# An attention and lookup block on one core: the first two heads' q and k loads reordered, split and spread

## What is computed

```python
x = x + layernorm(attention(layernorm(x)))     # 16 heads, D = 16, softmax over 4096 keys
x = x + layernorm(lookup_ffn(layernorm(x)))    # top 8 of 1024 keys, gated

def attention(x):                              # all in float32
    q, k, v = split(x @ w_qkv + b_qkv)
    attn = softmax((q @ k.T) * D ** -0.5)      # one 4096 x 4096 matrix a head
    return (attn @ v) @ w_proj + b_proj
```

## Time and profile before

| | us |
|---|---|
| median of 3 runs | 3294.21 |
| the runs | 3290.62, 3294.21, 3294.38 |
| the profiled execution | 3291.98 |
| its span | 3290.2 |

### The profile page before, as it was taken

One profiled execution on the slowest core, in us unless ns is written; L12 is line 12 of the kernel. 1 busy time (PEld: TensorE's weight loads), 2 busy tenths in 40 slices (PEclk: granted clock), 3 DMA queues, 4 the chain that ended last, 5 costly groups with the idle time before them and its releaser, 6 DMA issues.

```text
span 3290.2 us, 80364 instructions
## 1 busy us (share of the span) xinstructions
PE 3136.5 (95%) x27243; PEld 1406.9 (43%) x27243; DVE 2824.3 (86%) x3108; ACT 2514.8 (76%) x4551; POOL 262.0 (8%) x810
## 2 busy tenths in 40 slices
PE   8799999999999999999999999999999999988983
PEld 3444443444344434444444344434444444456662
DVE  5389998999899989998999899989999999456666
ACT  6158888888888888888888888888888888733333
POOL 2300000000000000000000000000000000011113
PEclk9689999999999999999999999999999999989996
DMA  7700101010110001010101010101010101000001
GB/s 255 90 1 1 30 11 27 14 27 14 21 21 21 21 18 24 18 24 15 27 11 30 8 33 8 33 5 37 5 37 5 36 1 30 1 0 0 0 0 51
DMA packets 27384, 83.26 MB, mean 25 GB/s; under 512 B 4641, under 2 KB 15633, under 8 KB 24018
## 3 DMA queue, kind: packets, MB, share of 16 engines
q1 hardware_dynamic: 26818, 77.84, 10.7%
q0 software_dynamic: 272, 1.05, 0.1%
HBM read 57.90 MB, written 20.97 MB: 24 GB/s over the span
## 4 chain that ended last, share of the span: by engine, by line
PE 94%; DVE 2%; issue 2%; ACT 1%; DMA 1%; POOL 1%; DVEq 0%; SPq 0%; POOLq 0%; ACTq 0%
PE ps L1023 41%; PE ps L1034 35%; PE ps L1253 4%; PE ps L998 3%; PE ps L1044 2%; PE ps L1202 2%; PE ps L957 2%; PE ps L1242 1%; PE ps L1177 1%; PE ps L971 1%; PE ps L1052 1%; PE ps L949 1%; DMA q_stack<-qk_parts 1%; ACT q_raw L619 1%; PE ps L1219 0%
## 5 line engine op out<-in xcount | busy, mean ns | idle before, releaser
L750 DVE TENSOR_REDUCE partial<-ps 128x1 f32<-128x1024 f32 x2048 | 2460.7, 1223 | 202.5 <-PE ps L998 158.5
L569 ACT ACTIVATE work<-ps 128x512 f32<-128x512 f32 x4096 | 2203.9, 598 | 383.0 <-PE ps L1023 173.9
L998 PE MATMUL ps<-k_stack,q_stack 48*128 48x512 f32 x4096 | 1509.4, 449 | 25.3 <-DMA q_stack<-qk_parts 17.0
L1023 PE MATMUL ps<-q_stack,k_stack 64*128 64x512 f32 x4096 | 1508.2, 448 | 18.8 <-issue 17.8
L1034 PE MATMUL ps<-work,v_head 128*32 128x256 f32 x16384 | 1304.4, 393 | 0.0
L1023 PEld LDWEIGHTS ps<-q_stack,k_stack 64*128 64x128 f32 x4096 | 633.0, 185 | 814.4 <-ACT work L569 695.6
L998 PEld LDWEIGHTS ps<-k_stack,q_stack 48*128 48x128 f32 x4096 | 622.6, 187 | 55.6 <-DVE partial L750 31.9
L1034 PEld LDWEIGHTS ps<-work,v_head 128*32 128x32 f32 x16384 | 330.9, 108 | 702.6 <-issue 436.8
L415 POOL CAST nm_parts<-negmax 128x4 bf16<-128x4 f32 x128 | 24.7, 193 | 2256.1 <-DVE negmax L757 2255.2
L1253 PE MATMUL ps<-k_raw,q_raw 128*128 128x256 f32 x512 | 126.3, 403 | 17.8 <-ACT q_raw L619 17.8
L619 ACT ACTIVATE q_raw<-ps 128x1024 f32<-128x1024 f32 x32 | 32.8, 1024 | 131.4 <-PE ps L1242 131.4
(11 more groups left out here) (128 smaller groups left out, 1137.4 us busy)
## 6 DMA issues: line engine op xcount, KB each, us to landing
k_stack<-qk_parts SPq DMA_DIRECT2D x96, 256.0 KB, 4.2
q_stack<-qk_parts SPq DMA_DIRECT2D x96, 256.0 KB, 4.2
qk_parts<-qk_part SPq DMA_DIRECT2D x32, 512.0 KB, 2.8
x_sb<-L_attn_x SPq DMA_DIRECT2D x8, 512.0 KB, 11.1
out<-work SPq DMA_DIRECT2D x8, 512.0 KB, 2.9
k_raw<-L_ffn_aux_values SPq DMA_DIRECT2D x1, 1024.0 KB
work<-L_attn_w_qkv POOLq DMA_DIRECT2D x1, 768.0 KB, 7.4
q_raw<-L_ffn_aux_keys SPq DMA_DIRECT2D x1, 512.0 KB
```

Source lines behind the costliest of these rows:

```text
L569: act.activation(probs[:, g % DEPTH, i, :], ps[:, bank, :], ACT.Exp, scale=SCALE).then_inc(exp_done, 1)
L750: dve.tensor_reduce(partial[:, k // 4, k % 4:k % 4 + 1], ps[:, 2 * slot:2 * slot + 2, :], AX.XY, ALU.max).then_inc(max_used, 1)
L998: last = pe.matmul(ps[:, 2 * slot + e, :], q_stack[HALF:HALF + ROWS, b1, c * CH + (k // 4) * P:c * CH + (k // 4 + 1) * P], k_stack[HALF:HA ...
L1023: pe.matmul(ps[:, bank, :], k_stack[0:HALF, b, P * tile:P * (tile + 1)], q_stack[0:HALF, b, at:at + CH], start=True, stop=True).then_inc(s ...
```

## The change

The first head's twelve loads are issued by a new function, `load_first`, in another order: slots 3, 4 and 5 (the maxima's rows) of both stacks first, counted on a new semaphore `first_max_in`, then slots 0, 1 and 2, counted on `first_score_in`. SP issues them after waiting for `parts_out[0]` and `parts_out[2]` only, and waits for `parts_out[1]` and `[3]` behind them. TensorE waits for `first_max_in` ahead of the first maxima and for `first_score_in` ahead of the first score unit. The second head's loads no longer follow at once: each waits on `pv_done`, the first for one finished unit of head 0's first iteration, each further one for two more. As the first head no longer counts on `stack_in[1]`, the loop's wait for it is one head lower.

```diff
--- before.py
+++ after.py
@@ -206,6 +206,8 @@
         v_evac = sem("v_evac")
         v_biased = sem("v_biased")
         stack_in = [sem(f"stack_in{b}") for b in range(NB)]
+        first_max_in = sem("first_max_in")
+        first_score_in = sem("first_score_in")
         s_ready = sem("s_ready")
         exp_done = sem("exp_done")
         m_ready = sem("m_ready")
@@ -296,19 +298,25 @@
                     dst = parts_dram[g // 2, :, (g % 2) * P:(g % 2 + 1) * P, bass.ds(c * CH, CH)]
                     sp.dma_start(dst.rearrange("r f t -> f r t"), qk_part[:, g, :, :]).then_inc(parts_out[g], 16)
 
-            for g in range(4):
-                sp.wait_ge(parts_out[g], 16 * (NC + 1))
-
-            def load_stack(h, b, after=None):
+            def load_first(slots, done):
+                for n in slots:
+                    for stack, qk, part in ((k_stack, 1, SLOT_K[n]), (q_stack, 0, SLOT_Q[n])):
+                        sp.dma_start(stack[SLOT_ROW[n]:SLOT_ROW[n] + D, 1, 0:T].bitcast(F32),
+                                     parts_dram[qk, part, 0:D, :]).then_inc(done, 16)
+
+            def load_stack(h, b, after):
                 for n, (row, pq, pk) in enumerate(zip(SLOT_ROW, SLOT_Q, SLOT_K)):
                     for m, (stack, qk, part) in enumerate(((k_stack, 1, pk), (q_stack, 0, pq))):
-                        if after is not None:
-                            sp.wait_ge(pv_done, after + (2 * n + m) * LOAD_EVERY)
+                        sp.wait_ge(pv_done, after + (2 * n + m) * LOAD_EVERY)
                         sp.dma_start(stack[row:row + D, b, 0:T].bitcast(F32), parts_dram[qk, part, h * D:(h + 1) * D, :]
                                      ).then_inc(stack_in[b], 16)
 
-            load_stack(0, 1)
-            load_stack(1, 0)
+            for g in (0, 2, 1, 3):
+                sp.wait_ge(parts_out[g], 16 * (NC + 1))
+                if g == 2:
+                    load_first((3, 4, 5), first_max_in)
+                    load_first((0, 1, 2), first_score_in)
+            load_stack(1, 0, 1 + CREDIT[pv_done])
             for h in range(2, H):
                 load_stack(h, (h + 1) % NB, (h - 1) * PAIRS * KG + CREDIT[pv_done])
 
@@ -1123,7 +1131,7 @@
                        (b, PAIRS - 1, chunks_ahead(b, PAIRS - 1)))
                 attend(first + (PAIRS - 1), b, PAIRS - 1, chunks_ahead(b, PAIRS - 1), (1 - b, 0, chunks_ahead(1 - b, 0)))
 
-            pe.wait_ge(stack_in[1], 16 * LOADS)
+            pe.wait_ge(first_max_in, 16 * LOADS // 2)
             for c in range(AHEAD):
                 for k in range(16):
                     for e in range(2):
@@ -1139,11 +1147,12 @@
             max_row(1, S_BANK[-1 % SRING])
             pe.wait_ge(vhead_ready, 1)
             pe.wait_ge(rows_set, 2)
+            pe.wait_ge(first_score_in, 16 * LOADS // 2)
             for g in range(LAG):
                 unit(g, 0, 1, 0, chunks_ahead(1, 0), None)
             with pe.Fori(0, H // NB - 1) as r:
                 next_loaded(r * NB, 1, r + 1)
-                next_loaded(r * NB + 1, 0, r + 2)
+                next_loaded(r * NB + 1, 0, r + 1)
             next_loaded(H - 2, 1, H // NB)
 
             def transpose_weights():
```

## The result

| | before | after |
|---|---|---|
| median, us | 3294.38 (6 runs, 3290.62 to 3295.13) | 3275.94 (6 runs, 3266.65 to 3277.40) |
| profiled execution, its span | 3291.98, 3290.2 | 3277.40, 3275.6 |

The ratio of after to before is 0.9941, 95% interval 0.9928 to 0.9954. The forecast was 3276.3.

A forecast was written before the change was run, and what follows sets the result against it. TensorE, busy 95% of the span, bounds the kernel, with 17.0 us idle awaiting the first loads. Cutting that by 15.6 us plus 0.9 us of clock gives 16.5, from 3292.8 to 3276.3 us; range 3270.5 to 3283.

The forecast's parts named there:

- Step 1: First head's loads: the maxima's six go first, the sixth landing 16.15 us after first issue; 13.9 us without the early issue.
- Step 2: SP's waits before the first head's loads: waiting for groups 0 and 2 only moves the first issue 1.7 us earlier.
- Step 3: Score rows' six loads: land 14 us later, at 114.4, at no cost, with 60 us of cover.
- Step 4: Second head's loads, spread over the first iteration: last issue near 243.4, price 0, cover 19 us.
- Step 5: TensorE's clock at the start of the maxima: first four matmuls take half of 2.07 us, gain 0.9 us.
- The sum: Whole change: 15.6 us of shorter TensorE idling plus 0.9 us of clock, 16.5 us.
- The fit: DMA skill page's transfer formula: twelve loads would take an estimated 9 us, so the change would give 0.
- B: Rival at the first loads: half of the gain, slower landings and 4 us lost to ScalarE or clock, 3283; chance 0.10.
- C: Rival at the first loads: twelve share the queue, only 1.7 us of early issue is left, 3291; chance 0.03.
- D: Rival at the third iteration: second head's loads late, TensorE waits 22 us plus 3.4 of clock, 3302; chance 0.02.
- A: Rival in the maxima: clock stays high, up to 24 us more gain, half priced, 3264; chance 0.07.

The follow-up runs named there:

- e1: Kernel before with only the new order and split of the first head's loads; median 3278.86 us, ratio to before 0.9965.
- e2: Kernel before with only the early issue, the first head's loads going out after groups 0 and 2; median 3292.02 us, ratio to before 1.0004.
- e3: Kernel before with only the second head's loads spread over the first iteration; median 3293.23 us, ratio to before 1.0000.
- e8: Changed kernel with the second head's loads let out nine units later; median 3282.98 us, ratio to before 0.9974.
- e6: Changed kernel with q's first 1024 columns of the maxima's rows loaded ahead of the other 3072; median 3273.60 us, ratio to before 0.9940.
- e11: Changed kernel with k's first two slots of each set loaded by one 512 KB transfer on 32 partitions instead of two; one run, 3273.89 us.
- e4: Changed kernel without the spreading, the second head's loads issued at once; median 3275.92 us, ratio to before 0.9948.
- e5: Changed kernel with each v unit among the maxima cut into two halves; median 3275.70 us, ratio to before 0.9934.
- e7: Changed kernel with both halved v units and q's first 1024 columns loaded first; median 3255.24 us, ratio to before 0.9889.
- e9: The kernel of e7 run again for more executions; median 3246.75 us, ratio to before 0.9869.

## Why the prediction was right

**Step 1**, order and split, was right and is most of the gain: e1. The sixth landing came 16.3 us after the first issue (86.72 + 14.1 against 84.46), where 16.15 was forecast.

**Step 2**, the early issue, was over-sized. The issue did move (84.46 against 86.05, with a profile that runs 0.2 us late), but only 1.0 us of the 1.7 reaches TensorE in e2, and 1.5 us between e1 and after. The prediction put the other bound at 0 and was right to keep one.

**Step 3** held: the score rows landed at 89.49 + 25.0 = 114.5, 62 us ahead of the first score at 176.2. (The prediction's "next 62 us" on the maxima's rows alone are 192.74 - 116.11 = 76.6 us by the earlier trace rows; nothing in the sum uses them.)

**Step 4** held: last issue at 243.83 (243.4 forecast), combines 41.3 us apart with the loads in the first iteration, no wait ahead of the third; e3 gives the price as 0 and e8 the cover.

**Step 5**, the clock. The 0.9 us is there: four maximum matmuls took 1.19 us and not 2.07. The v units before the wait were also faster, 14.07 us for 15.76, as the clock had not dropped at 84.6 in this execution. TensorE's idle stretch so came out at 3.2 us in place of 1.4 and the sum was not touched, since the start hangs on the landing. In e8's profile, the same program up to there, the clock did drop and the wait is 1.7 us, near the forecast.

**The sum** of 16.5 us is the first combine's 16.6, which is closer than that mark can tell: with e8's execution in place of after's it would be 18.5. That the time came out 0.4 us from the forecast is partly luck. The forecast started from 3292.8, the six executions of before have a median of 3294.38, so the measured gain is 18.4 us, 1.9 more than the sum. The range (3270.5 to 3283) held; 7.6 of its 12.5 us were bounds on the gain, the rest was for the scatter between executions. (Its own terms give 3292.8 - 19.6 - 2 = 3271.2 for the lower end.)

The fit that the prediction set against this change (the Trainium skill, "DMA: Bandwidth & Descriptors", section "Anatomy of one DMA") is the page's for transfers that GpSimd issues. The loads here are SP's. The 2.3 us a load decide the case, but they do not show that fit to be wrong where the page gives it.

**The rivals.** B's 4 us of clock and C did not come, D did not either, and e8 shows that its price was read nearly rightly, 1.3 us of clock too high. A, with a chance of 0.07, did not come in the changed kernel, and the prediction's reason against it, the fall at 125.55 "without any long gap", held for whole v units. With them the clock fell in every profile, and when it fell does not follow the wait: at 105.1 with none (e6), near 112 with 1.0 us (e11), at 107.1 with 1.6 (e4) and near 102 with 3.2 (after). With halved units e5, which waits for 1.9 us, has three executions of ten some 25 us under the others, and all nine of e7 and e9, which do not wait, are there, their profiles with the clock at 1.00 and e7's with the 4.9 us a step that the prediction had worked out. Whether the 1.9 us send e5 down its long course, or something else that varies between executions, was not separated. In the kernel as changed A came at most in part. One execution of six took 3266.65 us at a mean granted clock of 0.971, where the other five have 0.967 or 0.968; this can as well be the lookup part, which took 397.3 us at 0.89 in e8's profile and 406.5 at 0.87 after. The Trainium skill, "TensorE: Matmul & The Clock Gate", section "Why this matters for your kernels", warns of idle gaps between bursts, but of longer ones than e5's 1.9 us. This case's trace does not agree in full: in e5's profile the clock fell at 101.1, just behind that wait. The measurement decides.

## What to carry to other kernels

When an engine waits for a queue of equal transfers, count which of them it needs first, and find its start from the landing of the last of these in the trace; issuing the queue earlier and clearing what stands behind it were worth 1 to 1.5 us and 0 here, the order 14. Cutting the first transfer down to what the first steps read, and dividing filler work evenly, added to the change, brought the kernel to 0.9889 (e7) and 0.9869 (e9) of before, where the change alone has 0.9941. Neither edit did so alone: e6 did not, e5 in three executions of ten, and the granted clock of the stage is what differs. So check that clock over the stage behind any wait that an edit shortens. Judge an edit of the start by a mark right behind it, here the first combine, rather than by the end, where the untouched lookup part varies by 10 us, and take a second profile of the same program to see what the mark itself varies by, here 2 us.

## What the runs showed of the hardware

The same stage of maxima and halved v units went two ways: it ran at 0.50 in a stretch of 88.7 us with TensorE busy for 83.3 of them (e5), and at 1.00 in one of 54.5 us with 48.8 of them busy (e7). Within one kernel, e5, the times fall into two groups some 25 us apart. A TensorE that is busy nearly without a gap at half the clock did not get the full one back; it came only at 189.8, 2.6 us after the products with v had begun. That differs from what the Trainium skill's page on the clock gate has in the same section, that keeping TensorE busy gets it past the half rate: it did in the v units of before, at 88.0, and not here. Which property of the work decides was not tried.

A load of 16 rows of 16 KB takes 2.3 us of its queue whether it is alone in its transfer or half of one of 32 rows (e11), some 112 GB/s, and 16 rows of 4 KB take 0.6 us (e6), while a write of 512 KB from 128 partitions on the same queue landed 2.8 us after its issue in before.
